# Row maxima of a first attention layer 14 units ahead of the exponentials instead of 18, their turn one position later, and separate signals for the parts of queries and keys

## The reference

```python
def _L0_xattn_ref(zt_prev, za, Wq, Wk, Wv, Wo, ...):
    q = layer_norm(transpose(zt_prev + pos_enc), ln_q_g, ln_q_b)
    kv = layer_norm(transpose(za + pos_enc), ln_kv_g, ln_kv_b)
    Q = split(q @ Wq); K = split(kv @ Wk); V = split(kv @ Wv)      # 16 heads of 16
    attn = jnp.einsum('bhqd,bhkd->bhqk', Q, K) / math.sqrt(DH)
    ctx = jnp.einsum('bhqk,bhkd->bhqd', jax.nn.softmax(attn, axis=-1), V)
    r = merge(ctx) @ Wo + q
    h = layer_norm(r, ffn_ln_g, ffn_ln_b)
    return transpose(gelu(h @ W1 + b1) @ W2 + b2 + r)
```

## Time and profile before

| | us |
|---|---|
| runs of the kernel before | 1831.66, 1829.23, 1830.99 |
| their median | 1830.99 |
| the profiled execution | 1830.12 |
| its span, first to last instruction | 1828.3 |

### The profile page before, as it was taken

How to read it: one execution, slowest core, us unless ns; L and a number is a source line. 1 busy time by engine, 2 the same in 40 slices (tenths; PEclk the granted TensorE clock), 3 DMA queues, 4 the chain that set the end, 5 groups by cost and what they waited for, 6 DMA issues and landing times.

```text
span 1828.3 us, 32546 instructions
## 1 busy us (share of the span) xinstructions
PE 1708.0 (93%) x11840; PEld 1224.9 (67%) x11840; DVE 1206.6 (66%) x2792; ACT 1060.2 (58%) x2333; POOL 142.2 (8%) x207
## 2 busy tenths in 40 slices
PE   3879999999999988999999989999999799999999
PEld 2324343444434333788888878888887689999998
DVE  5666776767676552488888888888888653333332
ACT  2345666766666575587778877877777531111111
POOL 2110101101000000001000000000000100000000
PEclk8779999999999898999999999999999999999999
DMA  6322223222222222566656767666667330000000
GB/s 162 115 85 65 94 83 99 73 94 84 87 72 61 87 62 75 141 164 173 182 151 183 192 175 206 181 174 179 168 168 177 114 127 24 24 24 24 24 24 12
DMA packets 169479, 201.62 MB, mean 110 GB/s; under 512 B 25956, under 2 KB 117220, under 8 KB 169320
## 3 DMA queue, kind: packets, MB, share of 16 engines
q1 hardware_dynamic: 169032, 199.14, 38.9%
q10 hardware_dynamic: 288, 0.39, 0.2%
HBM read 131.84 MB, written 67.63 MB: 109 GB/s over the span
## 4 chain that ended last, share of the span: by engine, by line
PE 79%; DVE 10%; ACT 6%; issue 3%; DVEq 1%; DMA 1%; ACTq 0%; POOL 0%; SPq 0%
PE c_d L2121 10%; PE c_sums L2136 10%; PE b_d L1379 8%; PE b_d L1391 8%; PE a_d L499 6%; PE a_escore L472 5%; PE b_d L1458 5%; PE a_d L569 3%; PE a_d L577 3%; PE a_mscore L484 3%; PE a_d L553 3%; PE b_score L1446 3%; PE b_d L1475 2%; DVE a_mx L802 2%; DVE b_t L1781 2%
## 5 line engine op out<-in xcount | busy, mean ns | idle before, releaser
L802 DVE TENSOR_REDUCE a_mx<-a_mscore 128x2 f32<-128x1024 f32 x247 | 302.3, 1224 | 173.0 <-PE a_mscore L484 171.6
L639 ACT ACTIVATE a_pt<-a_escore 128x1024 f32<-128x1024 f32 x256 | 262.5, 1025 | 165.6 <-PE a_escore L472 165.4
L1605 ACT ACTIVATE b_pr<-b_t,b_nmax 128x256 f32<-128x256 f32 x512 | 254.4, 501 | 121.3 <-DVE b_nmax L1781 120.7
L2220 ACT ACTIVATE c_gT<-c_d,c_b 128x256 f32<-128x256 f32 x128 | 53.7, 472 | 267.7 <-PE c_d L2121 267.7
L1781 DVE CUSTOM_DVE_ANT_0 b_t<-b_t,b_minus 128x256 f32<-128x256 f32 x512 | 191.1, 429 | 16.9
L1777 DVE TENSOR_TENSOR b_t<-b_score,b_mask 128x1024 f32<-128x1024 f32 x128 | 154.9, 1210 | 65.2 <-PE b_score L1446 65.2
L472 PEld LDWEIGHTS a_escore<-a_qst,a_kst 50*128 50x128 f32 x512 | 50.0, 191 | 180.9 <-ACT a_pt L639 109.6
L472 PE MATMUL a_escore<-a_qst,a_kst 50*128 50x512 f32 x512 | 133.7, 518 | 24.7 <-ACT a_pt L639 23.5
L2265 DVE CAST c_g_high<-c_gT 128x512 fp32r<-128x512 f32 x64 | 40.2, 629 | 172.4 <-ACT c_gT L2220 172.4
L2121 PE MATMUL c_d<-c_ln_high,c_w_high 128*128 128x256 f32 x512 | 145.4, 284 | 2.4 <-DVE c_ln_low L2267 2.4
L2121 PE MATMUL c_d<-c_ln_high,c_w_low 128*128 128x256 f32 x512 | 145.6, 284 | 0.0
(11 more groups left out here) (166 smaller groups left out, 3248.6 us busy)
## 6 DMA issues: line engine op xcount, KB each, us to landing
b_qst<-b_q SPq DMA_DIRECT2D x96, 256.0 KB, 4.7
b_kst<-b_k SPq DMA_DIRECT2D x96, 256.0 KB, 6.4
b_q<-b_qparts SPq DMA_DIRECT2D x64, 256.0 KB, 4.2
b_k<-b_kparts SPq DMA_DIRECT2D x64, 256.0 KB, 3.6
a_qst<-a_q_parts SPq DMA_DIRECT2D x192, 64.0 KB, 2.2
a_kst<-a_k_parts SPq DMA_DIRECT2D x186, 64.0 KB, 2.2
a_k_parts<-a_kparts SPq DMA_DIRECT2D x32, 256.0 KB, 2.3
a_q_parts<-a_qparts SPq DMA_DIRECT2D x32, 256.0 KB, 2.3
```

The lines of the kernel that those rows point to most:

```text
L639: nc.scalar.activation(pt[:, at % RING, :, :], escore[:], ACT.Exp, scale=SCALE).then_inc(exp_done.sem, 1)
L802: nc.vector.tensor_reduce(mx[:, 2 * pair:2 * pair + 2, q], maxima_bank(b, n)[:], AX_X, ALU.max).then_inc(max_done.sem, 1)
L1605: last = nc.scalar.activation(pr[:, u % 2, j, :], t[:, u % 2, j, :], ACT.Exp, scale=-1.0, bias=nmax[:, u, j:j + 1], accum_out=esum[:, u, j ...
```

## The change

`LEAD` goes from 9 to 7, so the maxima run 14 units ahead. The turn of each group moves one position: step "m" from p0, p4, p8, p12 to p1, p5, p9, p13, and `negative_maxima` and `low_maxima` with it on ScalarE and VectorE. `parts_out` becomes two semaphores, one for the stores of the queries and one for those of the keys, and each wait names the one that it needs. No instruction is added or taken away on any engine except by waits; lines behind the edits are numbered one or two higher.

```diff
-    LEAD = 9
+    LEAD = 7
...
-        parts_out = [sig(f"parts_out{m}", 4, 16) for m in range(CT)]
+        parts_out = [[sig(f"{n}_out{m}", 2, 16) for m in range(CT)] for n in "qk"]
...
-            4: ["E0", "M0", ("m", 0, 2), ("pv", 0, 0, 0), ("pv", 0, 0, 1), "E1", "M1", ("pv", 0, 0, 2), ("pv", 0, 0, 3)],
-            5: ["E0", "M0", ("ctx", 0, 0), ("tok", 2, 1), "E1", "M1", ("chan", -1, 2)],
+            4: ["E0", "M0", ("pv", 0, 0, 0), ("pv", 0, 0, 1), "E1", "M1", ("pv", 0, 0, 2), ("pv", 0, 0, 3)],
+            5: ["E0", "M0", ("m", 0, 2), ("ctx", 0, 0), ("tok", 2, 1), "E1", "M1", ("chan", -1, 2)],
...
             def first_keys():
                 act.wait_ge(consts.sem, 1)
-                parts_out[0].need(act, 0, 4)
+                parts_out[1][0].need(act, 0, 2)
...
-                if p == 4:
+                if p == 5:
                     negative_maxima(i, 2)
...
                 if p == 4:
+                    apply(i - 1, 2)
+                if p == 5:
                     low_maxima(i, 2)
-                    apply(i - 1, 2)
```

More of the change, by code:

```diff
@@ L305, in free_early @@
                 qk_filled[m].need(eng, B - 1, 2)
-                parts_out[m].need(eng, B - 1, 4)
+                for s in range(2):
+                    parts_out[s][m].need(eng, B - 1, 2)
             for s in range(2):
@@ L366, in put @@
                     sp.dma_start((scratch_q, scratch_k)[s][b, part, m * P:(m + 1) * P, :],
-                                 parts[s][:, part, m, :].bitcast(F32)).then_inc(parts_out[m].sem, 16)
+                                 parts[s][:, part, m, :].bitcast(F32)).then_inc(parts_out[s][m].sem, 16)
             def stack(b, g):
@@ L379, in stack @@
                         continue
-                    parts_out[g // 2].need(sp, b, 4)
+                    parts_out[s][g // 2].need(sp, b, 2)
                     for e in range(2):
@@ L696, in high_part @@
                     return
-                parts_out[m].need(act, b - 1, 4)
+                parts_out[s][m].need(act, b - 1, 2)
                 qk_filled[m].need(act, b, 2 - s)
@@ L734, in position @@
                 exponentials(*unit_of_exp(i, p, 0))
-                if p == 0:
+                if p == 1:
                     negative_maxima(i, 1)
@@ L748, in position @@
                 if p == 8:
+                    gelu(i - 1)
+                if p == 9:
                     negative_maxima(i, 3)
-                    gelu(i - 1)
-                if p == 12:
+                if p == 13:
                     negative_maxima(i + 1, 0)
@@ L908, in position @@
                         nc.vector.memset(vaug[:, :, :, DH:DH + 1], 1.0).then_inc(consts.sem, 1)
-                if p == 8:
+                if p == 9:
                     low_maxima(i, 3)
```

## The result

| | us |
|---|---|
| kernel before, median of 8 runs | 1831.25 (1828.61 to 1831.66) |
| changed kernel, median of 8 runs | 1837.89 (1834.29 to 1840.71) |
| ratio, 95% interval | 1.0038, 1.0027 to 1.0049 |
| profiled execution of the changed kernel, its span | 1839.56, 1837.8 |

The changed kernel is slower: 0.38% by the ratio, 6.6 us between the medians. Its runs lie in two heaps, four between 1834.3 and 1836.2 and four between 1839.6 and 1840.7, and the median lies in the gap between them, where no run is. The profiled one is from the upper heap; two more of its executions were profiled later and are shown with the experiments.

A forecast was written before the change was run, and what follows sets the result against it. TensorE was taken to bound the middle of the first layer. Terms -7.0 + 4.5 + 4.9 + 0.4 + 4.5 = +7.3, plus 0.7 for p9, gave +8.0 us on 1830.99, so 1839.0 us, range 1831 to 1846.

The forecast's parts named there:

- first exponentials: Start of the kernel: first exponentials at 64.6 us in place of 71.65, -7.0 us, bounds -9.0 and -5.0.
- falls of the clock: Bodies 1 to 5 at p5: the clock falls in three of five, 1.5 us each, +4.5 us.
- seam: Four units of maxima move to p7 and p8 of body 7: +0.4 us, bounds 0 and +1.5.
- part on position 13: Bodies 0 to 5 at p13: "chan" waits for the low part, 0.8 us six times, +4.9 us in the sum.
- stall of the turn: Start, end of p13: the second "chan" waits for a maximum, its low part and "m", +2.0 us.
- Rival C: Start gives 3 us less because exponentials wait for transfer of group 0's maxima or first keys: 1842 us, chance 0.12.
- rests at p5 and p13: Transposes wait about 1.6 us at p5 (bodies 1 to 5) and 0.9 at p13 (bodies 0 to 5).
- VectorE's lag behind p5: Bodies 1 to 5: VectorE, held up at p5, makes TensorE's M0 wait at p8, 0.3 us each.
- Rival B: Middle bodies: new waits only replace old ones, a body costs 0.3 us, not 1.7: 1826.5 us, chance 0.09.
- sign of 82 us or more in bodies 1 to 5: Forecast's sign of being right: bodies 1 to 5 take 82 us or more in place of 80.06.
- Rival D: The clock falls at p13 too and stays low longer, five more falls at 1.5 us: 1846.5 us, chance 0.07.
- rival A: The stalls come but the clock holds in every body: 1834.5 us, within 0.2% of before, chance 0.22.

The follow-up runs named there:

- e9: The changed kernel run again without an edit: 1832.13 us (one run).
- e11: The kernel before run again without an edit: 1828.68 us (one run).
- E0: Not a run: the step that comes first in TensorE's order at positions such as p5 and p13; no time as a kernel.
- e10: The changed kernel run once more without an edit: 1834.15 us (one run).
- e7: The changed kernel with one signal again for all stores of query and key parts: 1835.40 us, ratio 1.0029.
- e4: The kernel before with LEAD = 8 and separate query and key signals, turns at their old positions: 1823.59 us, ratio 0.9965.
- e12: The changed kernel with VectorE's low part ahead of the second row maximum at p5 and p13: 1819.93 us, ratio 0.9946.
- e1: The changed kernel with the turn one or two steps later in the ring at both p5 and p13: 1822.86 us, ratio 0.9959.
- e5: The changed kernel with the turn two steps later in the ring at p5 alone: 1826.42 us, ratio 0.9982.
- e6: The changed kernel with the turn put behind the first "chan" at p13 alone: 1832.36 us, ratio 1.0012.
- e2: The changed kernel with LEAD = 9, so maxima 18 units ahead again: 1835.52 us, ratio 1.0031.
- e3: The kernel before with only the signals of query and key parts separated: 1827.92 us, ratio 0.9987.

## Why the prediction came out as it did

Predicted were 1839.0 us and a slower kernel; measured were 1837.89 and a slower kernel. The mechanism was right, and that the number is off by only 1.1 us is luck: the measured median lies in the gap between the heaps, and the sum is closer than its terms. Each term in the first trace, and in e9 against e11, which ran together:

| term | predicted | first trace | e9 - e11 |
|---|---|---|---|
| first exponentials | -7.0 | -5.9 | -7.3 |
| body 0 | +0.9 | +2.45 | +1.1 |
| bodies 1 to 5, rests | +9.0 | +6.5 | +6.7 |
| bodies 1 to 5, falls of the clock | +4.5 | +3.1 | +5.8 |
| body 6 | 0 | -0.7 | -0.8 |
| seam, to E0 of p9 in body 7 | +0.4 | +0.6 | -0.6 |
| behind that, to the end of the span | 0 | +3.5 | -1.4 |
| span | +8.0 | +9.5 | +3.5 |

The forecast's terms in this table add up to 7.8: its sum has 4.9 where six times 0.8 is 4.8, and 0.1 for body -1. It also adds 0.7 for p9, which the part on position 13 had called covered by the bounds. TensorE's wait at that E0 is 2.25 us in the changed kernel, 2.66 before. The row of the rests is five times what a body without a fall is longer by (81.36 - 80.06, and 81.39 - 80.06); the falls are what is left of the five bodies.

**The start: right in mechanism, the stall of the turn too large.** The first one's last step of the normalisation, the 4.9 us of the second and the wait of TensorE for VectorE came as worked out: the first row maximum starts at 39.52, forecast was 40.4, and TensorE's next maxima unit waits 4.10 us for it. From there to the first exponentials 24.2 us were forecast, and 26.2 (first trace), 23.8 (e9) and 25.4 (e10) were measured. In this the turn's stall was put at 2.0; from the first "chan" at p13 to the maxima behind the second it is 0.7 (5.19 us against 4.51 before). The rest goes with the clock. The second "chan" in the changed kernel, then the same projection shortly ahead of the first exponentials in it and in e9, at 1.2 and at 2.4 GHz:

```profile
54.23 1.12 PE L547 MATMUL a_d<-a_ident,a_tokn 128*128 128x128 f32 x4 [0.46 <-DVE a_mparts L839]
...
61.45 2.07 PE L554 MATMUL a_d<-a_qnT,a_wq 128*128 128x512 f32 x2
```

```profile
59.45 1.12 PE L554 MATMUL a_d<-a_qnT,a_wq 128*128 128x512 f32 x2
```

In e9 the first exponentials are 7.3 sooner than in e11, in e10 4.7, which is just outside the bounds of 5.0 and 9.0. What the signals add was taken as 1.7, and VectorE's queue shows 1.4 (e7). It was wrong to hold the start for a fixed number: it moves by 3 us in an unchanged kernel. Body 0, which runs at 0.76 of the clock, moves too: 85.67, 84.22 and 83.77 us in the three executions, so the +2.45 of the first trace is no price of the rest at p13. Rival C is out: in none of the three do the first exponentials wait for a transfer, as they do in e4.

**The rests at p5 and p13: right, but too much a body.** Forecast were rests of about 1.6 and 0.9 us at the transposes; 1.60 and 1.02 were measured. Body 3 by positions, each from its E0 to the next one's, against the kernel before:

| positions | forecast | changed | e12 |
|---|---|---|---|
| p0 | 0 | -0.21 | -0.21 |
| p1 to p3 | 0 | 0 | 0 |
| p4 to p6, the rest at p5 | +0.6 | +0.61 | -0.21 |
| p7 and p8 | +0.3 | +0.09 | -0.19 |
| p9 | +0.1 | +0.25 | +0.24 |
| p10 and p11 | 0 | -0.26 | -0.25 |
| p12 to p15, the rest at p13 | +0.8 | +0.82 | -0.12 |
| body 3 | +1.8 | +1.30 | -0.74 |

Both places come to what was forecast, p13 by luck: the rest there costs 1.02 from p13 to p15, 0.2 more than forecast, and p12, which the turn has left, is 0.2 shorter. The 0.3 for VectorE's lag behind p5 is there too, but doesn't show. Position 8 in the kernel before, in the changed one and in e12:

```profile
355.91:363.92 8.01, 8.01 (x48) 2.57 (x47) 3.90 (x7) 7.73 (x8) 4.70 (x2) 1.00 0.32 85
```

```profile
357.24:365.34 8.10, 8.08 (x48) 2.64 (x47) 4.20 (x7) 7.59 (x7) 5.12 (x3) 1.00 0.28 82
```

```profile
346.51:354.33 7.82, 7.82 (x48) 2.61 (x48) 3.87 (x7) 7.59 (x7) 4.79 (x3) 1.00 0.30 84
```

Without the lag (e12) p8 is 0.2 shorter than before, as the turn has left it; with the lag it is 0.28 longer than that, and so it is in e1, whose low part is as late. What the forecast missed is this: the turn takes TensorE's time at p0, p4, p8 and p12, 0.2 each, and its leaving was counted at p4 alone ("less a little"). Not counted were p0 and p8, and the 0.26 of p10 and p11, for which the rows show no cause. At p9 TensorE waits 0.21 us for VectorE's L832, more than the 0.1 forecast. Together a body costs 1.3 in place of 1.8. Rival B is out: the waits do not vanish in old ones beyond the 0.73 at "f1" that the forecast had counted, and 0.1 at p14. Against e5 and e1, with shorter waits of their own at these places, each rest costs 0.6 (81.36 - 80.78, 80.78 - 80.18).

**The falls: right.** Three of five at 1.5 us were forecast; the three traces of the changed kernel have two, three and three, costing 1.3 to 1.5 each, and 2.9 where the stretch was longer. The sign of 82 us or more in bodies 1 to 5 came in those bodies only; without a fall they take 81.4 to 81.7. e6 and e12 carry the reason: with the rest at p5 alone all five bodies have one, with 0.45 us there none has. Over bodies 1 to 5 of all profiled executions the clock fell behind p5 in 16 of 30 with the 1.6 us rest (changed kernel, e2, e6, e7, e9, e10), and nowhere in the 40 without it. Rival D, falls behind p13, is out: the rest of 1.0 us stands there in 30 bodies (the same executions with e5 in place of e6), and in none does the clock fall behind it.

The Trainium skill, in "TensorE: Matmul & The Clock Gate", section "Why this matters for your kernels", ties such drops to idle gaps longer than any here. The trace does not agree: a rest of 1.60 us stands right ahead of transposes at 1.2 GHz (263.08). By that rule, rival A, the three falls would have cost nothing; its 1834.5 lies near e9 and e10, but for other reasons, since both have their falls.

**What was left out: the clock behind the seam.** I counted nothing there, as the change touches nothing there. In the first trace it costs 3.5 us, 3.0 of them by a fall of the clock at the last "f2", behind a wait that has the same length in both kernels. At E0 of p9 in body 7 the changed kernel is 6.0 us behind, 2 less than forecast for the whole; what comes behind makes up for these 2 and adds 1.5. The misses cancel, and that is luck. The two later executions, 1832.13 and 1834.15 us, say the same: with them the median of ten is 1835.5, and they are 3 and 5 us above the runs of before beside them (1828.68 and 1828.89). So the loss that belongs to the change is nearer 5 us than 7. What decides when that wait lets the clock fall isn't settled.

## What to carry to other kernels

When a step that releases a shared buffer is moved, move it on every engine to the first place where its input is there, and not just to the same position: a 0.27 us instruction behind a 1.23 us one cost some 14 to 17 us here, clock included (the changed kernel against e12, each against its own runs of before). A step that is moved also gives back its own time where it was. Price a new rest of TensorE twice, once as the rest and once as a possible fall of the clock; the falls cost once to twice as much again as the rest at p5 itself (3.1 and 5.8 us, against five times 0.6). And where the granted clock moves by itself, profile the unchanged kernel more than once before a difference of 3 us in one trace is given a cause.

## What the runs showed of the hardware

- A rest of 1.6 us in an otherwise full TensorE is followed by the lower clock in 16 of 30 cases, one of 1.0 us in none of 30 and one of 0.45 us (e12) in none of five. The lower clock can set in right at the end of the rest (263.08, changed kernel) or 1.8 us behind it (343.55, e6).
- Where the clock falls differs between executions of one kernel: the start moves by 2.8 us (62.91 to 65.74), and sixteen matmuls take 7.13 us in some executions and 10.16 in others. The Trainium skill, in "TensorE: Matmul & The Clock Gate", section "What's actually happening", says that the number of slow matmuls at a kernel's start varies from run to run; the traces agree (two matmuls of L554 take 2.07 us in one execution and 1.12 in another), and show the same in the middle and at the end of the first layer.
- The loads of keys, issued 2.3 us sooner, gave TensorE its first maxima 3.7 us sooner (e3). Loads of two queues that no longer start together land faster: the six loads of keys take 2.3 us each from issue to landing (median) in e3 and 4.4 in the kernel before, the twelve of queries 2.2 and 5.1.
